# Local attention with contiguous keys, one maximum and one PT bank per half of the heads, and the mask as a TensorE product

## The reference, cut to what matters

```python
h = shift_token(x)
q, k, v = split(h @ wqkv)          # 8 heads of 64
q, k = l2norm(q) * qs, l2norm(k) * ksc
q, k = rotary_xpos(q, k)
# blocks of 64 rows; a block sees itself and the 64 rows before it
sim = einsum('bhwid,bhwjd->bhwij', 8 * q, k)
mask = (i < j) | (i > j + 64) | (j == -1)
attn = softmax(where(mask, -max, sim))
x = x + (attn @ v) @ wo
```

## Time and profile before

| | us |
|---|---|
| median of 3 runs (3113.74 to 3120.27) | 3114.63 |
| the profiled execution | 3112.19 |
| its span in the trace | 3110.1 |
| PE busy / DVE busy / ACT busy / POOL busy | 2916.1 / 2247.4 / 2181.2 / 1674.6 |
| mean granted TensorE clock | 0.981 of full speed |

### The profile page before, as it was taken

The page is one execution under the profiler, slowest core; times in us unless marked ns, Lnnn a source line. Parts: engine busy times, 40 slices in busy tenths (PEclk is TensorE's granted clock), DMA queues, the critical chain, the costliest instruction groups (busy, mean ns, idle before and its releaser), DMA issues. The chain is left out here.

```text
span 3110.1 us, 86020 instructions
## 1 busy us (share of the span) xinstructions
PE 2916.1 (94%) x24464; PEld 2099.8 (68%) x24464; DVE 2247.4 (72%) x7447; ACT 2181.2 (70%) x6591; POOL 1674.6 (54%) x2189
## 2 busy tenths in 40 slices
PE   6999999999999999996899999997889999999886
PEld 4666666666666666664677777775757777777575
DVE  5766776766676776765788888885568888888655
ACT  5766776766666766774788888884448888888642
POOL 3334444443344443433777778773257877777621
PEclk9999999999999999998999999999989999999998
DMA  1000000000000000001211111111111111111112
GB/s 63 7 7 8 8 8 9 5 9 7 7 8 9 8 8 6 8 5 45 72 26 27 27 27 27 24 26 43 30 25 28 27 26 25 27 27 27 38 31 71
DMA packets 125850, 71.42 MB, mean 23 GB/s; under 512 B 79684, under 2 KB 110224, under 8 KB 125584
## 3 DMA queue, kind: packets, MB, share of 16 engines
q1 hardware_dynamic: 123264, 66.02, 8.6%
q10 hardware_dynamic: 2320, 2.20, 0.2%
HBM read 17.58 MB, written 8.41 MB: 8 GB/s over the span
## 5 line engine op out<-in xcount | busy, mean ns | idle before, releaser
L282 POOL TENSOR_SCALAR L<-L,rinv 128x128 f32<-128x128 f32 (+3 forms) x1024 | 522.6, 532 | 759.4 <-DVE rinv L465 759.4
L348 ACT ACTIVATE L<-L,nmax 128x128 f32<-128x128 f32 (+3 forms) x1024 | 565.0, 556 | 12.4 <-DVE nmax L452 3.1
L452 DVE CUSTOM_DVE_ANT_0 L<-bank,bias_tab 128x128 f32<-128x128 f32 (+3 forms) x1024 | 473.3, 486 | 98.2 <-PE bank L568 93.8
L887 ACT ACTIVATE f_L<-f_L,f_nmax 128x128 f32<-128x128 f32 x1024 | 402.7, 394 | 111.3 <-DVE f_nmax L954 105.7
L954 DVE CUSTOM_DVE_ANT_0 f_L<-bank,f_mask,f_rq 128x128 f32<-128x128 f32 x1024 | 340.3, 350 | 95.8 <-PE bank L1060 59.4
L846 POOL TENSOR_TENSOR f_rn<-f_ssq,f_mhalf 128x16 f32<-128x16 f32 x128 | 373.2, 2915 | 0.0
L589 PE MATMUL bank<-ident,L 128*128 128x128 f32 x2560 | 355.6, 278 | 2.2 <-DVE PT L214 1.0
L589 PEld LDWEIGHTS bank<-ident,L 128*128 128x128 f32 x2560 | 291.3, 143 | 45.3 <-DVE PT L214 13.3
L214 DVE COPY PT<-bank 128x512 f32<-128x512 f32 x384 | 264.8, 690 | 56.8 <-PE bank L589 53.9
L607 PE MATMUL bank<-PT,v 128*64 128x512 f32 (+3 forms) x2048 | 303.9, 439 | 0.0
L214 ACT ACTIVATE PT<-bank 128x512 f32<-128x512 f32 x256 | 151.8, 593 | 183.0 <-PE bank L589 183.0
(11 more groups left out here) (153 smaller groups left out, 7708.4 us busy)
## 6 DMA issues: line engine op xcount, KB each, us to landing
f_vm<-f_v SPq DMA_DIRECT2D x192, 128.0 KB, 2.2
f_hs<-xf SPq DMA_DIRECT2D x132, 32.0 KB
f_hs<-xf SPq DMA_DIRECT2D x132, 31.8 KB
xb<-in_L_attn_x SPq DMA_DIRECT2D x16, 256.0 KB, 2.8
out<-yacc SPq DMA_DIRECT2D x32, 128.0 KB, 1.8
f_hs<-xf SPq DMA_DIRECT2D x32, 128.0 KB
out<-f_acc SPq DMA_DIRECT2D x4, 1024.0 KB, 7.5
f_hs<-xf SPq DMA_DIRECT2D x32, 127.0 KB
```

The costliest lines, as they stand in the source:

```text
L282: nc.gpsimd.tensor_scalar(t, t, rinv[:, h % RING, a, i:i + 1], 1.0, ALU.mult, ALU.mult).then_inc(s_N, 1)
L348: nc.scalar.activation(t, t, ACT.Exp, bias=nmax[:, p % RING, a, i:i + 1], scale=-1.0, accum_out=rsum[:, p % RING, a, i:i + 1]).then_inc(s_ ...
L452: nc.vector.tensor_tensor_reduce(out=L[:, p % RING, a, LOFF[i]:LOFF[i] + (i + 1) * P], in0=ps_s[a][i % 2][:, 0:(i + 1) * P], in1=bias_tab[ ...
L887: nc.scalar.activation(a, a, ACT.Exp, bias=nmax[:, ot % 2, h:h + 1], scale=-1.0, accum_out=rsum[:, ot % 2, h:h + 1]).then_inc(sem["exp"], 1)
```

## The change

- The key tile kT gets 64 columns of zeros ahead, so the 128 keys that a block of 64 rows sees lie next to each other; a mask of one kind per tile serves all heads. Values likewise: `vm` holds for each tile the block before it and its first block.
- Scores of all eight heads go to two PSUM banks, even heads in one and odd heads in the other. TensorE first writes the mask there (`ident_r` times mask, 512 columns), then adds 16 products of 64 by 64 by 128, in the order of the four quarters of the array.
- VectorE takes the maxima of each bank (four heads in one operation) and one product for nmax; ScalarE reads the scores from PSUM, with `rn` as scale and nmax as bias. The factor 8 is in the rotary table of q.
- Probabilities: even heads on GpSimd, odd heads on VectorE. Each bank is transposed as four heads and copied as 512 columns.
- q and k rotations lie in one buffer and are added together; their transposes come one slot later and keep their own banks.

```diff
+                pool.wait_ge(sem["rinv_even"], at(tb, TT, tt + 1))
+                a = L[:, tt % 2, 0]
+                nc.gpsimd.tensor_tensor(a, a, rinv[:, tt % 2, 0].unsqueeze(2).to_broadcast([P, FC, P]),
+                                        ALU.mult).then_inc(sem["probs_even"], 1)
...
+                pool.wait_ge(sem["q_products"], at(tb, TT, tt + 1))
+                pool.wait_ge(sem["k_products"], at(tb, TT, tt + 1))
+                pool.wait_ge(sem["qT_done"], at(tb, TT, tt - 1))
+                pool.wait_ge(sem["kT_done"], at(tb, TT, tt - 1))
                 for s in range(2):
-                    nc.gpsimd.tensor_tensor(halves(qr[:], s), halves(qa[:, r, :], s), halves(qb[:, r, :], 1 - s),
-                                            ALU.add).then_inc(sem["qr"], 1)
-                pool.wait_ge(sem["kab"], at(tb, TT, tt + 1))
-                pool.wait_ge(sem["kT_done"], at(tb, TT, tt))
-                for s in range(2):
-                    nc.gpsimd.tensor_tensor(halves(kr[:], s), halves(ka[:, r, :], s), halves(kb[:, r, :], 1 - s),
-                                            ALU.add).then_inc(sem["k_rotated"], 1)
...
-                pool.wait_ge(sem["logits"], at(tb, 8 * TT, 8 * (tt - 1)))
-                pool.sem_inc(w["gate_pool"], 1)
-                nc.gpsimd.tensor_scalar(rq8[:, r, :], rn[:, r, 0:FH], -8.0, 1.0, ALU.mult, ALU.mult).then_inc(sem["rq8"], 1)
...
-            def probs(h):
-                if four is None:
-                    return
-                tb, tt = four
-                act.wait_ge(sem["rinv"], at(tb, TT, tt + 1))
-                a = L[:, tt % 2, h, :]
-                nc.scalar.activation(a, a, ACT.Copy, scale=rinv[:, tt % 2, h:h + 1]).then_inc(sem["probs_act"], 1)
-            def exps(h):
+            def exps(a):
                 if three is None:
                     return
-                act.wait_ge(sem["logits"], at(ob, 8 * TT, 8 * ot + h + 1))
-                a = L[:, ot % 2, h, :]
-                nc.scalar.activation(a, a, ACT.Exp, bias=nmax[:, ot % 2, h:h + 1], scale=-1.0,
-                                     accum_out=rsum[:, ot % 2, h:h + 1]).then_inc(sem["exp"], 1)
+                ob, ot = three
+                act.wait_ge(sem["nmax"], at(ob, TT, ot + 1))
+                act.wait_ge(sem["PT_done"], at(ob, 2 * TT, 2 * (ot - 1)))
+                act.wait_ge(sem["rn"], at(ob, TT, ot + 1))
+                for k in range(FC):
+                    nc.scalar.activation(L[:, ot % 2, a, k, :], ps_s[a][:, k * P:k * P + P], ACT.Exp,
+                                         bias=nmax[:, ot % 2, a, k:k + 1], scale=rn[:, ot % 2, 2 * k + a:2 * k + a + 1],
+                                         accum_out=rsum[:, ot % 2, a, k:k + 1]).then_inc(sem["exp"], 1)
...
+            if four is not None:
+                evacuate_PT(act, nc.scalar.activation, four, 0, (ACT.Copy,))
             exps(0)
...
+                nc.scalar.activation(hT_hi[:, t % 2, :], ps_q[:, 0:P], ACT.Copy).then_inc(sem["hT_hi"], 1)
+            exps(1)
         tile_slots(act, slot)
...
-                nc.vector.tensor_tensor_reduce(out=L[:, ot % 2, h, :], in0=ps_s[h % 2][:, 0:P], in1=mask[:, min(ot, 1), :],
-                                               scale=rq8[:, ot % 2, h:h + 1], scalar=3.0e38, op0=ALU.add, op1=ALU.min,
-                                               accum_out=nmax[:, ot % 2, h:h + 1]).then_inc(sem["logits"], 1)
...
+            def maxima(a):
+                if three is None:
+                    return
+                ob, ot = three
+                dve.wait_ge(sem[("scores_even", "scores_odd")[a]], at(ob, TT, ot + 1))
+                if a == 0:
+                    dve.wait_ge(sem["nmax"], at(ob, TT, ot))
+                nc.vector.tensor_reduce(rmax[:, a, :], ps_s[a][:].rearrange("p (k j) -> p k j", k=FC), AX.X,
+                                        ALU.max).then_inc(sem["rmax"], 1)
...
+            inverse(1, four)
             if four is not None:
                 tb, tt = four
-                dve.wait_ge(sem["exp"], at(tb, 8 * TT, 8 * tt + 8))
-                nc.vector.reciprocal(rinv[:, tt % 2, :], rsum[:, tt % 2, :]).then_inc(sem["rinv"], 1)
-            sums(1, two)
-            table_product(3, two)
-            logits(0)
...
+                nc.vector.tensor_copy(kT[:, :, WIN + ot * P:WIN + ot * P + P],
+                                      ps_t[1][:].rearrange("p (c k) -> p c k", c=FC)).then_inc(sem["kT_out"], 1)
...
+            table_product(1, 0)
+            maxima(0)
+            maxima(1)
+            if three is not None:
+                dve.wait_ge(sem["rmax"], at(ob, 2 * TT, 2 * ot + 2))
+                dve.wait_ge(sem["rn"], at(ob, TT, ot + 1))
+                dve.wait_ge(sem["exp"], at(ob, 8 * TT, 8 * (ot - 1)))
+                nc.vector.scalar_tensor_tensor(out=nmax[:, ot % 2], in0=rmax[:], scalar=-1.0,
+                                               in1=rn[:, ot % 2, 0:FH].rearrange("p (k a) -> p a k", a=2),
+                                               op0=ALU.mult, op1=ALU.mult).then_inc(sem["nmax"], 1)
+            table_product(1, 1)
+            if four is not None:
+                evacuate_PT(dve, nc.vector.tensor_copy, four, 1)
...
+            sums(1)
+            inverse(0, three)
...
+            def scores():
+                if three is None:
+                    return
+                ob, ot = three
+                for a in range(2):
+                    pe.wait_ge(sem["exp"], at(ob, 8 * TT, 8 * (ot - 1) + 4 * a + 4))
+                    nc.tensor.matmul(ps_s[a][:].rearrange("p (k j) -> p k j", k=FC), ident_r[:],
+                                     mask[:, min(ot, 1), :].unsqueeze(1).to_broadcast([P, FC, P]), start=True, stop=False,
+                                     skip_group_check=True)
+                pe.wait_ge(sem["qT_out"], at(ob, TT, ot + 1))
+                pe.wait_ge(sem["kT_out"], at(ob, TT, ot + 1))
+                pe.sem_inc(w["gate_pe"], 1)
+                for k in range(FC):
+                    for half in range(2):
+                        for a in range(2):
+                            r, q, o = slice(DH * a, DH * a + DH), slice(WIN * half, WIN * half + WIN), ot * P + WIN * half
+                            last = nc.tensor.matmul(ps_s[a][q, k * P:k * P + P], qT[r, k, q], kT[r, k, o:o + P],
+                                                    start=False, stop=(k == FC - 1), skip_group_check=True)
+                            if k == FC - 1 and half == 1:
+                                last.then_inc(sem[("scores_even", "scores_odd")[a]], 1)
...
-            scores(0)
-            scores(1)
+            rotated_T(0)
+            rotated_T(1)
             if one is not None:
-                pe.wait_ge(sem["kab"], at(ib, TT, it))
+                pe.wait_ge(sem["sq"], at(ib, 2 * TT, 2 * it))
+                pe.wait_ge(sem["k_products"], at(ib, TT, it))
                 project(1, ps_k, one).then_inc(sem["qk_done"], 1)
+            scores()
+            probs_T(0)
+            probs_T(1)
```

More of the change, by code:

```diff
@@ L747, in local_attention, with evacuate_PT @@
     hT_hi, hT_lo, w_hi, w_lo = w["hT_hi"], w["hT_lo"], w["w_hi"], w["w_lo"]
[L748 to L755 removed]
+    sq, ssq, rn = w["sq"], w["ssq"], w["rn"]
+    ab, qkr, qT, kT, v, vm = w["ab"], w["qkr"], w["qT"], w["kT"], w["v"], w["vm"]
+    L, rmax, nmax, rsum, rinv, PT, OT = (w[n] for n in ("L", "rmax", "nmax", "rsum", "rinv", "PT", "OT"))
+    tab, mask, ident_r = w["tab"], w["mask"], w["ident_r"]
     block_ctx = nc.Block()
     block = block_ctx.__enter__()
[L760 removed]
+    def evacuate_PT(eng, copy, tile, a, how=()):
         tb, tt = tile
[L763 to L765 removed]
+        eng.wait_ge(sem["PT_done"], at(tb, 2 * TT, 2 * tt + a + 1))
+        eng.wait_ge(sem["pv_even"], at(tb, TT, tt))
+        eng.wait_ge(sem["pv_odd"], at(tb, TT, tt))
+        copy(PT[:, a].rearrange("p k q -> p (k q)"), ps_t[a][:], *how).then_inc(sem[f"PT_out{a}"], 1)
     @block.sync
@@ L976, in sums @@
+            def sums(k):
+                if one is None:
                     return
-                ib, it = tile
+                ib, it = one
                 dve.wait_ge(sem["sq"], at(ib, 2 * TT, 2 * it + 1 + k))
@@ new lines, in slot @@
+            table_product(0, 0)
+            if three is not None:
+                ob, ot = three
+                dve.wait_ge(sem["kT_done"], at(ob, TT, ot + 1))
+                for a in ("scores_even", "scores_odd"):
+                    dve.wait_ge(sem[a], at(ob, TT, ot))
+                nc.vector.tensor_copy(kT[:, :, WIN + ot * P:WIN + ot * P + P],
+                                      ps_t[1][:].rearrange("p (c k) -> p c k", c=FC)).then_inc(sem["kT_out"], 1)
+            table_product(0, 1)
@@ L1063, in transposes @@
-            def transposes(k):
+                if k == 0:
+                    pe.wait_ge(sem["rotated"], at(ob, 2 * TT, 2 * ot + 2))
+                    pe.wait_ge(sem["PT_out0"], at(ob, TT, ot - 1))
+                else:
```

(11 more changed lines are left out.)

315 lines of the change are left out of this document (108 added, 207 removed).

## The result

| | before | after |
|---|---|---|
| median of 4 runs | 3114.18 (3111.62 to 3120.27) | 3070.66 (3065.51 to 3073.86) |
| ratio, 95% interval | | 0.9856 (0.9835 to 0.9876) |
| the profiled execution | 3112.19 | 3073.86 |
| one tile | 9.93 | 9.52 |

What follows compares the result with a forecast made beforehand. The prediction saw a ring of engines waiting in turn, each with slack. After the change its longest ring summed to 10.75 us a tile against 9.93, times 128 +105 us, giving 3220 us; range 3080 to 3282.

Steps and rivals of the forecast that it cites:

- nmax waits for the power's end and the exponentials for nmax: VectorE's nmax starts only when GpSimd's power (2.92 us) ends, 0.03 us behind it; ScalarE's exponentials wait for nmax.
- the ring of 10.75 us: Forecast's longest chain per tile: GpSimd's products, sums and power, nmax, exponentials, v, hT copies, even inverse; 10.75 against 9.93 us.
- The odd probabilities: VectorE product of 512 columns, to get the shared port between GpSimd's two rotary sums, adding 0.39 us to the slot.
- the port that isn't held against nmax: Rival: nmax needn't wait for the power; a ScalarE, VectorE, TensorE ring of 9.66 us a tile, 3080 us; chance 0.20.
- The price of a single exponential: ScalarE, 128 columns read from PSUM with two pointer operands: 457 ns each, four with accumulator reads 1.86 us.
- The maxima and nmax: VectorE terms of the 9.66 us ring: two maxima over 512 columns 1.32 us, nmax 0.22 us.
- the 0.10 for double waits: Last term of the 9.66 us ring: 0.10 us a tile allowed for double waits.
- The rotary sums: GpSimd's two sums of 512 columns per tile, priced at 1.27 us each, ends 1.04 and 1.47.
- the scores' 1.16: TensorE term of the 9.66 us ring: four rounds of scores and their latency, 1.16 us.
- nothing is gained by work removed: Engines' work falls a little, ScalarE's by about 1 us; with 1.6 us of slack or more each, no gain by itself.
- At nothing: Items priced at zero: building masks and cleared edges, shifted value-row DMAs, filling and draining (five slots), MLP and causal attention.
- The rule of the shared port: VectorE instructions with two SBUF inputs and GpSimd's reading SBUF exclude each other for a whole instruction; nmax would wait too.

## Why the prediction was wrong

- **The step that failed**: "nmax waits for the power's end and the exponentials for nmax". It was drawn from ssq, which waited out L828 (and reads one tensor in SBUF, not two), and from L813 and L938, all beside GpSimd instructions of 256 columns or more. The power has 16 columns. It keeps the port for 0.15 us at most and runs for 2.9, and nmax starts inside it and takes 0.17. Only a power of 16 columns was run, so whether the few columns or the kind of operation frees the port stays open. Without that step the ring of 10.75 us, which hung on the power's whole length, isn't there.
- **The odd probabilities** were given a place between the two sums, with 0.39 us of GpSimd's time. They start just before the first sum and cost it 0.45. The size was nearly right, but it fell where GpSimd waits 1.4 us a tile for the even inverse anyway, so it costs nothing.
- **The rival that came true** is the port that isn't held against nmax (chance 0.20): 9.66 us and 3080 forecast, 9.52 and 3070.66 measured. The mechanism was right, and the sum is good partly by luck, since its errors cancel. The price of a single exponential was good (457 ns; 462), but the next starts 0.435 us after it, not 0.46, so the two groups were 0.23 us too dear. The maxima and nmax were 0.23 us too cheap (1.43 and 0.34, for 1.32 and 0.22), the square, the key copy and the scores by 0.10, and the 0.10 for double waits isn't seen.
- **The rotary sums** at 1.27 us are right (1.26 to 1.29 a sum where no product stands beside them), as is the scores' 1.16 (1.10 and a hand-off).
- **What the kernel before was bound by** was read wrongly. The prediction set TensorE's 39.5 of 39.74 us aside because ends of matmuls are modelled, and gave all engines slack. The starts follow each other without a gap, and the added matmul costs its full time: TensorE's work of 9.93 us was the tile. The change takes some 2 us of it away, and only 0.41 arrives, since the ring of the other engines stands at 9.52. The forecast of the time didn't rest on this, but its belief that nothing is gained by work removed did.
- **At nothing** held nearly. The two layers, from first hT_lo to last x_out, took 648.9 and 653.9 us before and take 628.1 and 627.7 now, 47 us less. 64 tiles of 9.52 are 609.5; the other 18 are filling and draining, where 13 and 17 stood before. The two executions shown differ by 38.3 us and the medians by 43.5: the 9 us between 38.3 and 47 lie outside the changed attention; what they are is not shown.
- **The rule of the shared port**: by the Trainium skill, SBUF — State Buffer, section "Who interferes with whom", a VectorE instruction with two SBUF inputs contends with a GpSimd instruction that reads SBUF, and the pair is locked for a whole instruction. The trace agrees for the 512-column instructions that met here (waits of 0.45 to 1.1 us in the rows shown), and for nmax of 8 columns against a sum or a key product. It doesn't agree for the power, which runs for 2.9 us and locks the pair for 0.15 at most.

## What to carry to other kernels

Look at TensorE's starts and waits, not at its busy time, to see whether it is the bound, and add one matmul: here it cost its own 0.23 us or nothing. When an instruction is said to hold a shared port, ask which instruction of its kind and size was seen to hold it, and for how long: here 16 columns held it for 0.15 us of 2.9. And a part that is moved off a ring gains only up to the next join. Add up the next ring before the move, as that of TensorE and VectorE at 8.92 us here, and ask what then starts sooner and what that meets, the DMA queue that waits for its result included.

## What the runs showed that was not expected

- GpSimd's power of 128x16 runs for 2.9 us and hinders VectorE's products with two SBUF inputs for 0.15 us at most, from its start (a product of 8 columns takes 0.156 us inside it and one of 512 columns 0.684, both as without it). Begun beside a running product, the power takes 3.36 to 3.39 us: it waits for the product, not the product for it.
- A VectorE product of 512 columns with both inputs in SBUF that begins beside GpSimd's running 512-column instruction waits for its end (1.14, 1.59 and 1.75 us in place of 0.69), and of two sums in a row for the one that runs, not for both. Which of the two comes first in a tile was decided by less than 0.1 us in the changed kernel.
- Exponentials with two pointer operands start 0.435 us apart though each takes 0.46; one pointer less makes that 0.345.
- The 16 score products of a tile (32 matmul rows) take 1.10 us when they go round the four quarters of the array, and 2.54 quarter after quarter.
- With the exponentials' ring shortened, the tile stopped at 8.92 us in two kernels, one with v ahead of the odd exponentials and one without: TensorE's and VectorE's own queues close a ring of that length, with TensorE never idle from the values to the scores.
